# Two-layer recurrence on one core: the first three gates summed in two halves, the last two after the products

## The chip, the cores and the metric

One core of a Trainium2 chip runs the whole program; the other cores are idle. The metric is the device time of one execution in microseconds (us). The engines are TensorE (PE, with its weight loads shown as PEld), VectorE (DVE), ScalarE (ACT), GpSimd (POOL) and SyncE (SP).

## The reference, cut to what matters

A small network of several blocks is computed; the change touches only the fourth, a two-layer LSTM-like recurrence over 126 positions, batch 16, state 256.

```
def _run_layer(x_seq, Wx, Wh, b):
    gx = x_seq @ Wx + b                      # [128 or 256] -> 5 gates of 256
    def step(carry, gx_t):
        h, c, m = carry
        g = gx_t + h @ Wh
        i, f = sigmoid(g[:, 0:256]), sigmoid(g[:, 256:512])
        c_tilde = tanh(g[:, 512:768])
        o = sigmoid(g[:, 768:1024])
        m_new = tanh(g[:, 1024:1280])
        c_new = f * c + i * c_tilde
        h_new = o * tanh(c_new) + m_new
        return (h_new, c_new, m_new), h_new
h1 = _run_layer(x, Wx0, Wh0, b0)
h2 = _run_layer(h1, Wx1, Wh1, b1)            # then a dense layer on h2
```

The blocks before it (patch embedding, attention, a routed feed-forward net) and after it (a second routed net) are the same in both kernels.

## The kernel before

**Layout.** Features lie on the 128 partitions. The five gates of 256 make ten chunks of 128 features (`GCH = 10`); chunks 0 to 5 (`XCH = 6`) are the input, forget and candidate gates (called IFC), chunks 6 to 9 the output gate and the memory gate (OM). All numbers of a matmul are split into a high and a low fp16 part. A chunk of one step takes 32 columns of PSUM: 16 for the products with the high part and 16 for those with the low part, which VectorE adds. Two steps (`PAIR = 2`) share a pair of PSUM banks x and y: before the change x holds the six IFC chunks and y the four OM chunks. Layer 0 has four banks (named bank in the profile), layer 1 the other four (named quad), so each layer has two pairs that alternate.

**Order of the work.** Both layers run in one loop, layer 1 four steps behind layer 0 (`BEHIND = 4`). `wave` unrolls the first 8 and the last values of t and makes a hardware loop of 4 steps a turn for the 116 in between. In t = 4 to 125 both layers work; in each of these 122 steps the kernel goes through two mirrored halves, one in which layer 0's state is finished and its next matmuls start, and one for layer 1. This text calls each a half-step.

**TensorE** (`both` in `rec_pe`, order by hand): `own(0)`: wait for the high part of the state (`high0`), 12 matmuls with the low weights on IFC (L1475), wait for the whole state (`state0`), 12 with the high weights (L1468), signal `pre_x0`; then 8 and 8 for OM, signal `pre_y0`. Then fillers that don't depend on this step: on even t the bias of the next pair (2 matmuls, L1494) and 12 matmuls of `chunks`; on odd t 8 of `chunks` and 10 of `from_first`, the input product of layer 1. Then the same for layer 1, `own(1)`, followed by 2 and 12 (even t) or 18 (odd t) fillers of `from_first`. So a half-step holds 40 matmuls of its own and 14 or 18 fillers.

**VectorE** (`both` in `rec_dve`): for layer l, with l' the other layer, in this order: `sum_part` x of layer l (L1644, 192 values read, 96 written per partition), then for l' `new_state` (L1672, output gate times tanh of the cell), `store_state` (L1683 the high part, L1685 the whole in f32), `store_low` (L1690, the low part, which completes the state), then for l again `sum_part` y (L1644, 128 read, 64 written), `products` (L1652), `new_cell` (L1658). Eight instructions in a half-step. Each has a wait of its own in front.

**ScalarE** (`both` in `rec_act`): `gates_x` (L1582, tanh of IFC, waits for sum x), `gate_out` (L1587, sigmoid of the output gate, waits for sum y), `cell_of` (L1595, tanh of the new cell, waits for the cell), `memory` (L1590). The order in the queue is not altered by the change: the output gate already stands ahead of the cell.

**GpSimd** copies layer 1's state to a history (L1417) and splits the next two inputs (L1402, L1405), for which it waits on `pre_y0` of an earlier step.

Of the kernel before, what the change touches and what calls it, by code (L numbers as in the profile page):

```python
# [30 lines left out]
SEQ = PATCHES + WORDS  # L31
# [26 lines left out]
XCH = 3 * KH  # L58
XW = XCH * BATCH
# [35 lines left out]
def build(nc, taps_in, patches_in, txt_in, cols_in, const_in, dense_in, qkvw_in, outw_in, heads_in, w0_in,  # L95
# [6 lines left out]
    with ExitStack() as ctx:  # L102
# [1351 lines left out]
        def rec_pe(pe):  # L1454
# [3 lines left out]
            def chunk_at(l, q, m, first, steps):  # L1458

                x, y = pair_banks(l, q)  # L1460
                to, at = (x, m * 64) if m < XCH else (y, (m - XCH) * 64)
# [22 lines left out]

            IFC, OM, TOP = range(XCH), range(XCH, GCH), range(1)

# [4 lines left out]
            def start_bias(l, q):  # L1491
                x, y = pair_banks(l, q)
                for to, lo, n in ((x, 0, XCH), (y, XCH, GCH - XCH)):
# [4 lines left out]
            def own(l, n, u, states):  # L1498
# [6 lines left out]
                for k in range(KH):  # L1505
                    mm = high_weights(l, q, w + k, states[k], odd, IFC)
                mm.then_inc(sg(f"pre_x{l}"), 1)
# [5 lines left out]


            def connect(n, k):

                j, part = FC_PARTS[n]
                if k == 0:
                    pe.wait_ge(sg("fcw_in"), 16)
                    pe.wait_ge(sg("hist"), (j * BLK + part.stop + BATCH - 1) // BATCH)  # L1520
                    pe.wait_ge(sg("sum_x0"), SEQ - 2 if j < 2 else SEQ)
# [9 lines left out]
            chunks(0, 0, WX0, xcur_parts[:, 0], IFC).then_inc(sg("pre_x0"), 1)  # L1531
# [4 lines left out]
            def both(t, u):  # L1536
                q, odd = u // PAIR, u % PAIR
                if here(t, 1, SEQ - 1):
                    before = (u - 1) % 4
                    own(0, t, u, [hpair0[:, before // PAIR, k, before % PAIR:before % PAIR + 1] for k in range(KH)])  # L1540
# [6 lines left out]
                if odd and here(t, PAIR, SEQ + 1):  # L1547
                    from_first(q, 0, OM)
                    from_first(q, 1, TOP)
                if here(t, BEHIND + 1, SEQ + BEHIND - 1):  # L1550
                    own(1, t - BEHIND, u, [hpair1[:, 1 - odd, k:k + 1] for k in range(KH)])
                if here(t, PAIR, SEQ + 1):
# [10 lines left out]
                    else:  # L1563
                        for which, name in ((IFC[1:], "pre_x1"), (OM, "pre_y1")):
                            mm = from_first(q, 1, which)
                            if isinstance(t, int) and t == PAIR + 1:
                                mm.then_inc(sg(name), 1)
                for j, k in FC_AFTER.get(t, ()) if isinstance(t, int) else ():
# [8 lines left out]
        def rec_act(act):  # L1577
            act.activation(warm[:, :], warm[:, :], ACT.Sigmoid)

            def gates_x(l, n):  # L1580
                act.wait_ge(sg(f"sum_x{l}"), n)
# [38 lines left out]
        def rec_dve(dve):  # L1620
# [18 lines left out]
            def sum_part(l, n, u, name):  # L1639

                x, y = pair_banks(l, u // PAIR)
                src, first, count = (x, 0, XCH) if name == "x" else (y, XCH, GCH - XCH)
                dve.wait_ge(sg(f"pre_{name}{l}"), n)
# [3 lines left out]
                                  ).then_inc(sg(f"sum_{name}{l}"), 1)  # L1647
# [45 lines left out]
            def both(t, u):  # L1693
# [5 lines left out]
                if first_layer:  # L1699
                    sum_part(0, n0, u, "x")  # L1700
# [4 lines left out]
                if first_layer:  # L1705
                    sum_part(0, n0, u, "y")
# [4 lines left out]
                if first_layer:  # L1711
                    products(0, n0)
# [473 lines left out]
```

## Time and profile before

| | |
|---|---|
| median of 3 runs | 999.2 us (995.4 to 1002.92) |
| profiled execution, its own time | 1000.61 us |
| its span, first to last instruction | 998.8 us |
| busy over the span | PE 849.3 (85%), PEld 681.8 (68%), DVE 762.0 (76%), ACT 506.2 (51%), POOL 367.3 (37%) |
| the stage of the change, both layers at work | from about 492.8 to 892.6 us |

The rows further down come from this one profiled execution. In a timeline row stand start, duration, engine, line, operation, tiles written and read, partitions times elements, how many instructions were merged, and in brackets idle time of the engine before it with what ended it. A duration runs from an instruction's start to its result; two instructions on VectorE or ScalarE that don't wait for each other overlap, so what an engine is really taken up by is the distance from one start to the next.

### The profile page before, as it was taken

The page shows a single profiled execution, that of the slowest core. Times are in us where ns is not written, and L with a number is a line of the kernel's source. Part 1 is how long each engine was busy: PE and PEld are TensorE (multiplying, and loading weights), DVE is VectorE, ACT ScalarE, POOL GpSimd, SP SyncE. Part 2 cuts the span into 40 slices and gives each one's busy share as a digit, 9 for nine tenths or more (in the row PEclk, how much of TensorE's full clock was granted, in tenths as well). Part 3 has the DMA queues.
Part 4 walks back from the last instruction along what each step waited for, and adds up shares of the span by engine and source line. Part 5 has one row for each costly group of instructions (what it writes and reads, how often), then busy time and mean ns, then how long its engine had stood idle before and what let it go on. Part 6 is the DMA issues. An engine that isn't in the chain of part 4 may idle for free.

```text
span 998.8 us, 44167 instructions
## 1 busy us (share of the span) xinstructions
PE 849.3 (85%) x17239; PEld 681.8 (68%) x17239; DVE 762.0 (76%) x2780; ACT 506.2 (51%) x1605; POOL 367.3 (37%) x565
## 2 busy tenths in 40 slices
PE   4577777735999999995899999999999999998595
PEld 2246554513666666662699999999999999985263
DVE  4447897598877777677789999999999999987144
ACT  0435776701765555653455555555555555556083
POOL 0305664656677777760011111111111111100644
PEclk8767997755999999995899999999999999999697
DMA  7710002420122222225200000000000000002133
GB/s 235 293 37 1 1 1 76 152 68 25 37 76 79 79 78 78 77 47 171 93 4 0 0 0 0 0 0 0 0 0 0 0 0 0 0 3 65 42 100 113
DMA packets 30137, 50.64 MB, mean 51 GB/s; under 512 B 7969, under 2 KB 19161, under 8 KB 30074
## 3 DMA queue, kind: packets, MB, share of 16 engines
q1 hardware_dynamic: 23578, 36.95, 11.7%
q0 software_dynamic: 6496, 12.84, 4.8%
q8 instruction: 40, 0.66, 0.3%
q14 instruction: 23, 0.19, 0.1%
HBM read 38.40 MB, written 11.38 MB: 50 GB/s over the span
## 4 chain that ended last, share of the span: by engine, by line
DVE 29%; PE 6%; issue 6%; ACT 5%; POOL 4%; DMA 1%; DVEq 1%; SPq 0%; POOLq 0%
DVE post L1644 7%; ACT post L1595 5%; DVE post L1672 5%; DVE post L1683 4%; DVE post L1658 4%; DVE post L1652 3%; DVE post L1685 3%; POOL y_scratch L1783 2%; POOL x_scratch L1777 1%; DVE post L1690 1%; PE quad L1468 1%; PE quad L1475 1%; PE bank L1475 1%; PE bank L1468 1%; PE bank L1523 1%
## 5 line engine op out<-in xcount | busy, mean ns | idle before, releaser
L1475 PE MATMUL quad<-post,area 128*128 128x16 f16 (+1 forms) x3760 | 174.2, 172 | 6.8 <-DVE post L1683 6.8
L1468 PE MATMUL quad<-post,area 128*128 128x32 f16 (+1 forms) x3760 | 175.8, 182 | 0.1
L1417 POOL COPY post<-post 128x32 f32 (+1 forms) x126 | 29.8, 237 | 336.2 <-DVE post L1690 336.2
L1475 PEld LDWEIGHTS quad<-post,area 128*128 128x128 f16 x3760 | 136.5, 96 | 16.1 <-DVE post L1683 12.5
L1475 PE MATMUL bank<-post,area 128*128 128x16 f16 (+1 forms) x3130 | 135.5, 171 | 3.8 <-DVE post L1683 2.1
L1468 PE MATMUL bank<-post,area 128*128 128x32 f16 (+1 forms) x3130 | 138.2, 180 | 0.1
L1468 PEld LDWEIGHTS quad<-post,area 128*128 128x128 f16 x3760 | 133.9, 96 | 0.2 <-issue 0.2
L1587 ACT ACTIVATE post<-post 128x32 f32<-128x32 f32 x252 | 57.8, 229 | 147.6 <-DVE post L1644 147.2
L1475 PEld LDWEIGHTS bank<-post,area 128*128 128x128 f16 x3130 | 106.5, 96 | 10.3 <-DVE post L1683 2.8
L1468 PEld LDWEIGHTS bank<-post,area 128*128 128x128 f16 x3130 | 106.1, 96 | 0.8 <-issue 0.3
L892 POOL DMA_INDIRECT y_scratch<-area x78 | 81.3, 1042 | 31.4 <-issue 18.0
L887 POOL DMA_INDIRECT area<-x_scratch,area x78 | 78.7, 1010 | 28.1 <-issue 21.0
L1644 DVE TENSOR_REDUCE post<-bank 128x96 f32<-128x192 f32 x252 | 80.6, 320 | 10.4 <-PE bank L1468 10.1
L1076 ACT ACTIVATE area<-quad 128x512 f16<-128x512 f32 x78 | 46.6, 598 | 76.4 <-PE quad L971 76.3
L1582 ACT ACTIVATE post<-post 128x96 f32<-128x96 f32 x252 | 71.3, 283 | 26.3 <-DVE post L1644 23.8
L1644 DVE TENSOR_REDUCE post<-quad 128x96 f32<-128x192 f32 x252 | 80.6, 320 | 2.4 <-PE quad L1468 1.8
L1273 DVE TENSOR_TENSOR area<-quad,area 128x512 f16<-128x512 f32 x78 | 53.6, 688 | 29.0 <-ACT area L1076 28.7
L1595 ACT ACTIVATE post<-post 128x32 f32<-128x32 f32 x252 | 57.8, 229 | 33.5 <-DVE post L1658 2.2
L1289 DVE SCALAR_TENSOR_TENSOR area<-bank,area 128x512 f32<-128x512 f32 x78 | 53.7, 688 | 27.0 <-ACT area L1087 14.9
L961 PE MATMUL bank<-w0s,area 128*128 x156 | 60.4, 387 | 0.2
L962 PE MATMUL bank<-w0s,area 128*128 x156 | 60.1, 386 | 0.0
L963 PE MATMUL bank<-w0s,area 128*128 x156 | 60.1, 386 | 0.0
(337 smaller groups left out, 1938.6 us busy)
## 6 DMA issues: line engine op xcount, KB each, us to landing
w0s<-in_w SPq DMA_DIRECT2D x12, 768.0 KB
area<-in_rec SPq DMA_DIRECT2D x7, 640.0 KB
post<-y_scratch SPq DMA_DIRECT2D x8, 504.0 KB
area<-in_w SPq DMA_DIRECT2D x4, 768.0 KB
area<-in_f SPq DMA_DIRECT2D x2, 1024.0 KB, 7.6
area<-in_patches SPq DMA_DIRECT2D x1, 1488.4 KB
x_scratch<-post SPq DMA_DIRECT2D x1, 1472.0 KB, 7.2
area<-in_taps SPq DMA_DIRECT2D x1, 1350.0 KB
```

Of the source, the lines that this page charges most:

```text
L887: pool.indirect_dma_start(xg[:, i % XG, :], None, x_dram, bass.IndirectOffsetOnAxis(src_row[:, i:i + 1].bitcast(mybir.dt.uint32), 0)).then ...
L892: pool.indirect_dma_start(y_dram, bass.IndirectOffsetOnAxis(dst_row[:, i:i + 1].bitcast(mybir.dt.uint32), 0), y_sb[:, i % YR, :], None).th ...
L961: pe.matmul(out, xh, wh, start=True, stop=False, skip_group_check=True)
L962: pe.matmul(out, xl, wh, start=False, stop=False, skip_group_check=True)
L963: pe.matmul(out, xh, wl, start=False, stop=True, skip_group_check=True).then_inc(sg(name), 1)
L1289: dve.scalar_tensor_tensor(out=hid[:, i % 2, :], in0=up_bank(i), scalar=HID_SCALE / (H_SCALE * W_SCALE), in1=silu[:, i % 2, :], op0=ALU.mu ...
L1468: mm = pe.matmul(chunk_at(l, q, m, first, operand.shape[1]), rec_w[:, w, 0, m * P:(m + 1) * P], operand, start=False, stop=False, skip_gro ...
L1475: mm = pe.matmul(chunk_at(l, q, m, first, operand.shape[1])[:, :, 0, :], rec_w[:, w, 1, m * P:(m + 1) * P], operand[:, :, 0, :], start=Fal ...
L1582: act.activation(gates[:, l, 0:3 * SW], pre[:, l, 0:3 * SW], ACT.Tanh, scale=UNSCALE).then_inc(sg(f"gates{l}"), 1)
L1587: act.activation(gates[:, l, OUT:OUT + SW], pre[:, l, 3 * SW:4 * SW], ACT.Sigmoid, scale=UNSCALE)
L1595: act.activation(tanh_c[:, l], gates[:, l, CELL:CELL + SW], ACT.Tanh, scale=0.5).then_inc(sg(f"tanh_c{l}"), 1)
L1644: dve.tensor_reduce(pre[:, l, first * BATCH:(first + count) * BATCH].rearrange("p (m b) -> p m b", b=BATCH), src[:, 0:count * 64].rearrang ...
```

## The change

The two PSUM banks of a pair are filled differently: x now holds only chunks 0 to 2 (`BCH = 3`), y holds chunks 3 to 5 and, behind them, 6 to 9.

- TensorE: in `own`, the 12 high-weight matmuls on IFC are done in two parts, first the six of chunks 3 to 5 (`SOONER`), then the six of chunks 0 to 2 (`LATER`), each with a signal on `pre_x`. The 16 OM matmuls move to `own_rest`, behind the fillers, and `own_rest` first waits until VectorE has summed the first half ("a") of this step, because OM writes the bank that this sum reads. In `from_first` the order of the chunks is changed to match. Matmuls and their sizes are the same in number; only the bias's two are 96 and 224 columns in place of 192 and 128 (x and y hold 3 and 7 chunks).
- VectorE: `sum_part` x becomes two sums, "a" (chunks 3 to 5, bank y) and "x" (chunks 0 to 2, bank x), each 96 read and 48 written. The order after `store_low` is products, sum y, new cell in place of sum y, products, new cell. Nine instructions in a half-step in place of eight.
- ScalarE: only the value that `gates_x` waits for doubles.

```diff
+BCH = XCH // 2
@@ chunk_at
-                to, at = (x, m * 64) if m < XCH else (y, (m - XCH) * 64)
+                to, at = (x, m * 64) if m < BCH else (y, (m - BCH) * 64)
@@ rec_pe
+            LATER, SOONER = range(BCH), range(BCH, XCH)
@@ start_bias
-                for to, lo, n in ((x, 0, XCH), (y, XCH, GCH - XCH)):
+                for to, lo, n in ((x, 0, BCH), (y, BCH, GCH - BCH)):
@@ own
                 pe.wait_ge(sg(f"state{l}"), n)
-                for k in range(KH):
-                    mm = high_weights(l, q, w + k, states[k], odd, IFC)
-                mm.then_inc(sg(f"pre_x{l}"), 1)
+                for part in (SOONER, LATER):
+                    for k in range(KH):
+                        mm = high_weights(l, q, w + k, states[k], odd, part)
+                    mm.then_inc(sg(f"pre_x{l}"), 1)
+
+            def own_rest(l, n, u, states):
+
+                q, odd, w = u // PAIR, u % PAIR, (WH0, WH1)[l]
+                pe.wait_ge(sg(f"sum_x{l}"), n * 2 + 1)
                 for k in range(KH):
                     low_weights(l, q, w + k, states[k], odd, OM)
                 for k in range(KH):
                     mm = high_weights(l, q, w + k, states[k], odd, OM)
                 mm.then_inc(sg(f"pre_y{l}"), 1)
@@ connect
-                    pe.wait_ge(sg("sum_x0"), SEQ - 2 if j < 2 else SEQ)
+                    pe.wait_ge(sg("sum_x0"), 2 * (SEQ - 2 if j < 2 else SEQ))
@@ both (TensorE)
                 if odd and here(t, PAIR, SEQ + 1):
                     from_first(q, 0, OM)
                     from_first(q, 1, TOP)
+                if here(t, 1, SEQ - 1):
+                    own_rest(0, t, u, states0)
                 if here(t, BEHIND + 1, SEQ + BEHIND - 1):
-                    own(1, t - BEHIND, u, [hpair1[:, 1 - odd, k:k + 1] for k in range(KH)])
+                    own(1, t - BEHIND, u, states1)
...
-                        for which, name in ((IFC[1:], "pre_x1"), (OM, "pre_y1")):
+                        for which, name in ((OM, "pre_y1"), (SOONER, "pre_x1"), (LATER[1:], "pre_x1")):
                             mm = from_first(q, 1, which)
                             if isinstance(t, int) and t == PAIR + 1:
                                 mm.then_inc(sg(name), 1)
+                if here(t, BEHIND + 1, SEQ + BEHIND - 1):
+                    own_rest(1, t - BEHIND, u, states1)
@@ gates_x (ScalarE)
-                act.wait_ge(sg(f"sum_x{l}"), n)
+                act.wait_ge(sg(f"sum_x{l}"), n * 2)
@@ sum_part (VectorE)
-                src, first, count = (x, 0, XCH) if name == "x" else (y, XCH, GCH - XCH)
-                dve.wait_ge(sg(f"pre_{name}{l}"), n)
+                src, first, count = {"x": (x, 0, BCH), "a": (y, BCH, XCH - BCH), "y": (y[:, (XCH - BCH) * 64:], XCH, GCH - XCH)}[name]
+                if name == "y":
+                    dve.wait_ge(sg(f"pre_y{l}"), n)
+                else:
+                    dve.wait_ge(sg(f"pre_x{l}"), n * 2 - 1 if name == "a" else n * 2)
@@ both (VectorE)
                 if first_layer:
+                    sum_part(0, n0, u, "a")
                     sum_part(0, n0, u, "x")
...
                 if first_layer:
-                    sum_part(0, n0, u, "y")
+                    products(0, n0)
...
                 if first_layer:
-                    products(0, n0)
+                    sum_part(0, n0, u, "y")
                     new_cell(0, n0)
                 if second_layer:
+                    sum_part(1, n1, u, "a")
                     sum_part(1, n1, u, "x")
...
                 if second_layer:
-                    sum_part(1, n1, u, "y")
+                    products(1, n1)
...
                 if second_layer:
-                    products(1, n1)
+                    sum_part(1, n1, u, "y")
                     new_cell(1, n1)
```

## Rows read from the trace of the kernel before

**Rows 1.** Page, busy time of each engine; and the lines of the chain that ended last

```profile
PE 849.3 (85%) x17239; PEld 681.8 (68%) x17239; DVE 762.0 (76%) x2780; ACT 506.2 (51%) x1605; POOL 367.3 (37%) x565
...
DVE post L1644 7%; ACT post L1595 5%; DVE post L1672 5%; DVE post L1683 4%; DVE post L1658 4%; DVE post L1652 3%; DVE post L1685 3%; POOL y_scratch L1783 2%; POOL x_scratch L1777 1%; DVE post L1690 1%; PE quad L1468 1%; PE quad L1475 1%; PE bank L1475 1%; PE bank L1468 1%; PE bank L1523 1%
```

**Rows 2.** Windows, the two-layer stage: stretch, length, busy (instructions), PEclk, DMA share, GB/s

```profile
492.80:892.60 399.80, 392.63 (x13562) 379.83 (x13562) 364.92 (x1946) 209.26 (x973) 55.19 (x240) 1.00 0.00 0
```

**Rows 3.** Waits, 500 to 880 us: who waited for whom, us in total, times, longest

```profile
ACT post L1587 <- DVE post L1644: 139.8, 231, 0.7
...
DVE post L1644 <- PE bank L1468: 9.0, 30, 0.4
```

**Rows 4.** Timeline of VectorE, one half-step (layer 1's state, then layer 0's)

```profile
665.42 0.19 DVE L1683 SCALAR_TENSOR_TENSOR post<-post 128x32 f16<-128x32 f32 x1
665.53 0.18 DVE L1685 SCALAR_TENSOR_TENSOR post<-post 128x32 f32<-128x32 f32 x1
665.75 0.19 DVE L1690 TENSOR_TENSOR post<-post 128x32 f16<-128x32 f32 x1
665.86 0.28 DVE L1644 TENSOR_REDUCE post<-quad 128x64 f32<-128x128 f32 x1
666.06 0.21 DVE L1652 SCALAR_TENSOR_TENSOR post<-post 128x64 f32<-128x64 f32 x1
666.31 0.19 DVE L1658 SCALAR_TENSOR_TENSOR post<-post 128x32 f32<-128x32 f32 x1
666.50 0.36 DVE L1644 TENSOR_REDUCE post<-bank 128x96 f32<-128x192 f32 x1
666.79 0.19 DVE L1672 SCALAR_TENSOR_TENSOR post<-post 128x32 f32<-128x32 f32 x1
667.02 0.19 DVE L1683 SCALAR_TENSOR_TENSOR post<-post 128x32 f16<-128x32 f32 x1
```

**Rows 5.** Timeline of ScalarE, the same half-step

```profile
666.17 0.23 ACT L1587 ACTIVATE post<-post 128x32 f32<-128x32 f32 x1 [0.59 <-DVE post L1644]
666.53 0.23 ACT L1595 ACTIVATE post<-post 128x32 f32<-128x32 f32 x1
666.67 0.21 ACT L1590 ACTIVATE post<-post 128x32 f32<-128x32 f32 x1
666.89 0.28 ACT L1582 ACTIVATE post<-post 128x96 f32<-128x96 f32 x1
```

**Rows 6.** Timeline of the weight loads, the same half-step, 58 of them

```profile
665.66 0.36 PEld L1475 LDWEIGHTS bank<-post,area 128*128 128x128 f16 x12
665.99 0.37 PEld L1468 LDWEIGHTS bank<-post,area 128*128 128x128 f16 x12
666.29 0.27 PEld L1475 LDWEIGHTS bank<-post,area 128*128 128x128 f16 x8
...
666.69 0.17 PEld L1475 LDWEIGHTS bank<-post,area 128*128 128x128 f16 x4
...
667.14 0.10 PEld L1468 LDWEIGHTS quad<-post,area 128*128 128x128 f16 x1
667.26 0.36 PEld L1475 LDWEIGHTS quad<-post,area 128*128 128x128 f16 x12
```

**Rows 7.** Timeline of the matmuls, the twelve with high weights on IFC

```profile
666.00 0.47 PE L1468 MATMUL bank<-post,area 128*128 128x32 f16 x12
```

**Rows 8.** Timeline of VectorE where its loop turns

```profile
662.83 0.19 DVE L1658 SCALAR_TENSOR_TENSOR post<-post 128x32 f32<-128x32 f32 x1
663.33 0.36 DVE L1644 TENSOR_REDUCE post<-bank 128x96 f32<-128x192 f32 x1 [0.30 <-PE bank L1468]
663.60 0.18 DVE L1672 SCALAR_TENSOR_TENSOR post<-post 128x32 f32<-128x32 f32 x1
```

**Rows 9.** Groups by line and form, VectorE, 500 to 880 us: the two kinds of sum

```profile
L1644 DVE TENSOR_REDUCE post<-bank 128x96 f32<-128x192 f32 x115 | 41.1, 357 | 9.1 <-PE bank L1468 9.0
L1644 DVE TENSOR_REDUCE post<-quad 128x64 f32<-128x128 f32 x116 | 32.7, 282 | 0.0
```

**Rows 10.** Timeline of VectorE after the recurrence: two instructions that both read PSUM

```profile
927.83 1.28 DVE L1992 SCALAR_TENSOR_TENSOR post<-bank,post 126x512 f16<-126x512 f32 x2
```

**Rows 11.** Timeline of VectorE in a step where layer 1 works alone

```profile
893.64 0.19 DVE L1683 SCALAR_TENSOR_TENSOR post<-post 128x32 f16<-128x32 f32 x1
...
894.72 0.69 DVE L1644 TENSOR_REDUCE post<-quad 128x96 f32<-128x192 f32 x2 [0.56 <-PE quad L1468]
895.42 0.23 DVE L1652 SCALAR_TENSOR_TENSOR post<-post 128x64 f32<-128x64 f32 x1
895.68 0.19 DVE L1658 SCALAR_TENSOR_TENSOR post<-post 128x32 f32<-128x32 f32 x1
```

More of the change, by code:

```diff
@@ L1530, in rec_pe @@
             pe.wait_ge(sg("xcur"), PAIR)
-            chunks(0, 0, WX0, xcur_parts[:, 0], IFC).then_inc(sg("pre_x0"), 1)
+            chunks(0, 0, WX0, xcur_parts[:, 0], SOONER).then_inc(sg("pre_x0"), 1)
+            chunks(0, 0, WX0, xcur_parts[:, 0], LATER).then_inc(sg("pre_x0"), 1)
+            pe.wait_ge(sg("sum_x0"), 1)
             chunks(0, 0, WX0, xcur_parts[:, 0], OM).then_inc(sg("pre_y0"), 1)
@@ L1537, in both @@
                 q, odd = u // PAIR, u % PAIR
+                before = (u - 1) % 4
+                states0 = [hpair0[:, before // PAIR, k, before % PAIR:before % PAIR + 1] for k in range(KH)]
+                states1 = [hpair1[:, 1 - odd, k:k + 1] for k in range(KH)]
                 if here(t, 1, SEQ - 1):
-                    before = (u - 1) % 4
-                    own(0, t, u, [hpair0[:, before // PAIR, k, before % PAIR:before % PAIR + 1] for k in range(KH)])
+                    own(0, t, u, states0)
                 if here(t, 0, SEQ - 3):
@@ L1646, in sum_part @@
                                       "p (m s g b) -> p s m b g", m=count, s=PAIR, g=2)[:, u % PAIR], AX, ALU.add
-                                  ).then_inc(sg(f"sum_{name}{l}"), 1)
+                                  ).then_inc(sg(f"sum_y{l}" if name == "y" else f"sum_x{l}"), 1)
             def products(l, n):
@@ L1718, in both @@
                     store_state(0, n0, u)
+                if first_layer:
                     store_low(0, n0, u)
                 if second_layer:
-                    sum_part(1, n1, u, "y")
+                    products(1, n1)
                 if isinstance(t, int) and t < NBLK:
```

## The prediction

> **What bounds the kernel now.** I read the page first. No engine is busy for the whole span, and the chain that ended last names VectorE's recurrence lines before all others, with ScalarE's L1595 among them [rows 1]. Then the windows: the stage with both layers at work lasts 399.8 us and VectorE starts 1946 instructions in it, which at eight a half-step is 243; by the code it is 122 steps of two, 244 [rows 2]. One half-step so takes 1.64 us. In this stage the matmuls look 98% busy, but that is a reading of overlapping matmuls, so it settles nothing: the timelines do.
>
> The timeline of VectorE shows what a half-step is made of. I write all times from H, the start of the high part (L1683), and take distances from start to start [rows 4]: high to whole state 0.11, to low part 0.22, to sum y 0.11, to products 0.20, to cell 0.25, to new state (L1672) 0.48 to 0.49, to the next high 0.22 to 0.23. The sum is 1.60 (665.42 to 667.02). What counts is why each distance has its length. 0.11 and 0.20 are VectorE's own pace for instructions that don't wait for each other; they fit elements read / 0.96 per ns plus 0.07 to 0.08 (32: 0.11; 128: 0.20; 192: 0.27 to 0.28 from the sum x to L1672 [rows 4, 8]). 0.22 and 0.25 are a full duration plus about 0.04: the next instruction needs this one's result. The 0.48 from cell to new state is ScalarE: the cell is done at +0.19, L1595 starts at +0.22, takes 0.23, and L1672 starts 0.03 to 0.04 later [rows 4, 5]. VectorE fills this gap with the sum x of the other layer.
>
> TensorE is close behind. The high part is done at H+0.19, the low-weight matmuls start at H+0.24; the state is done at H+0.52, the high-weight ones start at H+0.57 and end at 666.47 = H+1.05 [rows 6, 7]; sum x starts at H+1.08. Its 58 weight loads of the half-step go at 25 to 27 ns each: 12 in 0.33 (with a few hundredths of waiting for the state), 12 in 0.30, 16 in 0.40, 18 fillers in 0.48 to 0.50 (666.69 to 667.17, and the next load could start by 667.19). That is 1.52, and the next start is 1.60 after the first [rows 6]. So TensorE has 0.08 to spare, and in half-steps with 14 fillers rather more. It is granted 1.00, its 2.4 GHz level, throughout [rows 2]; nothing here alters that.
>
> Once a turn of the loop VectorE loses about 0.3: cell to sum x takes 0.50, and cell to new state 0.77 [rows 8]; 30 such waits make 9.0 us [rows 3]. 244 x 1.60 + 28 x 0.28 = 398, which is the stage. So the model of before closes.
>
> **The change, part by part, for one half-step.**
>
> *Order sum y, products, cell becomes products, sum y, cell.* Before: 0.11 + 0.20 + 0.25 = 0.56 from low part to cell. After: low part to products 0.11, products (64 elements) to sum y 0.07 + 0.075 = 0.145, sum y to cell 0.20, in which the products' result (0.21 + 0.04 = 0.25) has come: 0.455. Saved 0.105. This takes a wait for its own result off VectorE. The products need ScalarE's `gates_x` earlier by 0.20; sum x ends at H+1.44, the gates run to about H+1.75, the products are wanted at H+1.60+0.44: cover of 0.29 [rows 4, 5].
>
> *The output gate against the cell on ScalarE.* The output gate starts 0.31 after the start of sum y [rows 4, 5]. Before, the cell's tanh came 0.36 later still. Now the cell starts 0.20 after sum y, so its tanh could start at 0.42, but the output gate has only just started at 0.31, and ScalarE's pace for two such is 0.14 (L1595 to L1590 [rows 5]): 0.45. Cost 0.03, cell to new state becomes 0.52. Bounds: 0 and, if a sigmoid and a tanh don't overlap at all, 0.31 + 0.23 - 0.42 = 0.12. I take 0.03, by the nearest rows.
>
> *One sum more.* 192 elements in one piece cost 0.27 to 0.28; two of 96 cost 2 x (0.10 + 0.07) = 0.34. They lie in the gap that ScalarE sets. With C for the cell's start: "a" at C+0.14, "x" at C+0.31, VectorE free at C+0.48; wanted at C+0.52. Cost nothing, with 0.04 of cover; without it, all of the 0.06 to 0.07. That two sums from PSUM overlap like others is not seen before, the nearest is a pair of L1992, 512 read each, 1.28 for both at 0.67 each: 0.61 apart, 0.53 + 0.08 [rows 10]. Upper bound: no overlap, "a" takes its whole duration, 0.282 less 32 x 1.17 ns = 0.245 by [rows 9], then VectorE is free at C+0.55 and 0.03 is lost.
>
> The Trainium skill speaks against this part: VectorE: DVE Perf Modes (section on the TRN2 errata) gives an instruction that reads PSUM 120 cycles beside its elements, and its rules for kernel authors say to minimize the count of operations. By that figure, taken as an estimate, two sums would hold VectorE for 0.45, and the new state would start at C+0.56 to 0.59; the half-step 1.565 to 1.595 and the time 992 to 999. The rows above, at 0.07 to 0.08 beside the elements, don't agree with it as a pace.
>
> *TensorE, first half sooner.* "a" needs only six of the high-weight matmuls: H+0.57 + 0.125 + 0.19 = H+0.89, so it may start at H+0.92; VectorE wants it at C+0.11 with C = H+0.79, that is H+0.90. "x" may start at H+1.08 and is wanted at H+1.09. Both fit.
>
> *TensorE, the new wait.* Behind `own`'s 24 matmuls (to H+0.87) now come the fillers (to H+1.36), then `own_rest`. It waits for "a", done at H+0.92 + 0.25, seen 0.05 later: H+1.22. The fillers cover it by 0.14. Queued behind it are 16 matmuls (to H+1.76), and behind these the next `own`, which the next half-step wants at H+1.77. Cost nothing, but cover of 0.01 to 0.04 only. Bound: a second start from a wait costs 0.05 like the others, then TensorE's loop is 1.57.
>
> *Sum y* of this layer needs `own_rest`: last matmul H+1.76 + 0.19, wanted at H+1.53 + 0.585 = H+2.11. Cover 0.15. GpSimd's wait on `pre_y0` is for a step further back, and its input is used by fillers that run 0.40 earlier; no DMA is moved.
>
> *Where the loop turns*, the 0.3 before the first sum stays; "a" comes late, `own_rest(0)` with it, but VectorE is later still. Nothing. In steps with one layer alone (four at each end) the cell starts at H+2.04 [rows 11]; by the same distances after the change it is H+2.04 to 2.08. Nothing.
>
> **The sum.** 0.22 + 0.11 + 0.22 + 0.11 + 0.145 + 0.20 + 0.52 = 1.525, against 1.60. TensorE's loop, 1.52, just lets it. 0.075 x 244 = 18.3 us. From the profiled execution's own 1000.6 that is 982.3; this one lay 1.4 above the median of 999.2. I predict 982.
>
> **Rivals.**
>
> *More (975).* ScalarE's order costs nothing: 0.105 x 244 = 25.6 off. For it, the output gate is off the path of before by a third of a microsecond; against it, the queue is in order. 8%.
>
> *Less, by the sums (about 990).* Two PSUM sums in a row don't overlap: 0.245 + 0.17 from C+0.14 puts the new state at C+0.55, 0.045 x 244 = 11 us are left. For it: no such pair stands in the recurrence before; against it, the pair that overlaps [rows 10]. 10%. The rule of the skill quoted above would make this rival true, and larger.
>
> *Less, by TensorE (about 993).* Its loop is 1.57, the new wait costing 0.05: 0.03 x 244 = 7 us are left. For it: two engines would sit within 0.01 of each other, and neither can smooth the other's hiccups. 14%.
>
> *No change (999).* Two such losses, or a sigmoid before a tanh that doesn't overlap (1.62 in place of 1.525). 10%.
>
> *Slower (from 1009).* TensorE becomes the bound. Its order now has three waits a half-step in place of two, each of which empties what it had lined up. Where the waits of before ended, it lost 0.05. If `own_rest` resumed 0.125 or more late in every half-step, its loop would be over 1.645 and the kernel 0.045 x 244 = 11 us slower; it decides from 0.08, where 1.60 is reached. For it: 1.52 of 1.60 is used already. Against it: fillers of 0.48 lie between the last matmul that "a" needs and the wait. 9%.
>
> **How the numbers follow.** My forecast (977 to 987) has 49%. Faster by over 1% (about what a measurement here can tell from no change), below 989.2, takes it, "more", and some 6 of the 24 of the two "less": 0.63. Within 1%: their rest, no change: 0.28. Slower 0.09. The range reaches from "more" to no change, 975 to 999; the forecast's own is 977 to 987.
>
> **What would show it.** In the profile after, half-steps of 1.52 to 1.53 from L1683 to L1683; products to sum y 0.145; cell to new state 0.52 with the cell's tanh 0.14 behind the output gate; two sums 0.17 apart; no idle time of weight loads ahead of `own_rest`. Wrong: sums 0.25 apart; weight loads of 58 in over 1.55 with VectorE idle ahead of "a"; idle TensorE that ends on the sum.

## The result and the profile after

| | before | after |
|---|---|---|
| median | 998.0 us (4 runs) | 976.2 us (4 runs, 974.8 to 978.0) |
| ratio | 1 | 0.9763, 95% interval 0.9731 to 0.9794 |
| profiled execution's own time | 1000.6 us | 974.8 us |
| its span | 998.8 us | 973.0 us |
| from the high part of layer 0's fourth state to the last of the two-layer stage | 402.4 us | 378.0 us |
| the same, median distance of neighbouring high parts | 1.60 us | 1.50 us (mostly 1.49 and 1.50) |

The change is faster by 2.4% (2.2% by the quotient of the two medians). The forecast was 982, 18.3 us off the profiled execution of before. The direction was right, but the gain was larger: 24.4 us in the stage of the change. What was measured, 974.8 in the profiled execution and 976.2 in the median, lies just below the forecast's own range of 977 to 987. The rest of this text is on why.

The windows of the stage (length, busy of PE, PEld, DVE, ACT, POOL with instructions, granted clock) against [rows 2]:

```profile
491.20:866.60 375.40, 373.27 (x13577) 369.22 (x13578) 348.18 (x2188) 182.62 (x973) 53.44 (x240) 0.99 0.00 0
```

399.8 us became 375.4, 24.4 less, with 2188 instructions on VectorE, nine for each of 243 half-steps. The span fell by 25.8. Of the other 1.4, 2.3 us came ahead of the recurrence (its first high part stands at 479.79 in place of 482.04), where nothing was changed and where the other runs of this text on chips as fast there lie between 478.3 and 482.9, and 1.2 went the other way in the steps with one layer alone. So the change itself is worth about 23 us.

The timeline of VectorE after, one half-step, to be read against [rows 4]:

```profile
644.00 0.19 DVE L1701 SCALAR_TENSOR_TENSOR post<-post 128x32 f16<-128x32 f32 x1
644.11 0.18 DVE L1703 SCALAR_TENSOR_TENSOR post<-post 128x32 f32<-128x32 f32 x1
644.32 0.19 DVE L1708 TENSOR_TENSOR post<-post 128x32 f16<-128x32 f32 x1
644.43 0.22 DVE L1670 SCALAR_TENSOR_TENSOR post<-post 128x64 f32<-128x64 f32 x1
644.57 0.28 DVE L1662 TENSOR_REDUCE post<-bank 128x64 f32<-128x128 f32 x1
644.77 0.18 DVE L1676 SCALAR_TENSOR_TENSOR post<-post 128x32 f32<-128x32 f32 x1
644.92 0.42 DVE L1662 TENSOR_REDUCE post<-quad 128x48 f32<-128x96 f32 x2
645.26 0.19 DVE L1690 SCALAR_TENSOR_TENSOR post<-post 128x32 f32<-128x32 f32 x1
645.49 0.19 DVE L1701 SCALAR_TENSOR_TENSOR post<-post 128x32 f16<-128x32 f32 x1
```

From the high part H: state instructions as before, products at H+0.43, sum y at +0.57, cell at +0.77, the first half sum at +0.92, both halves together 0.42 from start to result, the new state at +1.26, the next high part at +1.49. The two sums overlap: 0.42 less one's 0.25 puts them 0.17 apart.

ScalarE in the same half-step, against [rows 5]: output gate, tanh of the cell, memory, gates.

```profile
644.88 0.23 ACT L1602 ACTIVATE post<-post 128x32 f32<-128x32 f32 x1 [0.72 <-DVE post L1662]
645.02 0.21 ACT L1610 ACTIVATE post<-post 128x32 f32<-128x32 f32 x1
645.14 0.21 ACT L1605 ACTIVATE post<-post 128x32 f32<-128x32 f32 x1
645.38 0.28 ACT L1597 ACTIVATE post<-post 128x96 f32<-128x96 f32 x1
```

TensorE's weight loads, against [rows 6]: twelve low, twelve high, fillers, the sixteen of `own_rest`, the next twelve.

```profile
644.25 0.37 PEld L1476 LDWEIGHTS quad<-post,area 128*128 128x128 f16 x12
644.57 0.36 PEld L1469 LDWEIGHTS quad<-post,area 128*128 128x128 f16 x12
644.86 0.17 PEld L1476 LDWEIGHTS quad<-post,area 128*128 128x128 f16 x4
...
645.35 0.28 PEld L1476 LDWEIGHTS quad<-post,area 128*128 128x128 f16 x8
645.55 0.27 PEld L1469 LDWEIGHTS quad<-post,area 128*128 128x128 f16 x8
645.75 0.37 PEld L1476 LDWEIGHTS bank<-post,area 128*128 128x128 f16 x12
```

There is no gap ahead of `own_rest` (645.35): the fillers cover its wait. TensorE goes round in 1.50, without rest: 0.32 + 0.29 + 0.49 + 0.40. Accordingly the page's chain that ended last now follows TensorE nearly all the way:

```profile
PE 41%; DVE 4%; POOL 3%; DMA 2%; issue 2%; ACT 1%; ACTq 0%; SPq 0%; POOLq 0%; DVEq 0%
PE quad L1469 11%; PE quad L1476 9%; PE bank L1469 9%; PE bank L1476 8%; POOL x_scratch L1798 2%; POOL y_scratch L1804 1%; DMA post<-y_scratch 1%; PE bank L1496 1%; PE quad L1496 1%; DVE post L1662 1%; DVE post L1318 0%; ACT area L1983 0%; PE bank L1530 0%; PE quad L1019 0%; DVE post L1926 0%
```

This reads as if TensorE's amount of work were now the bound. The experiments show that it isn't alone: two other chains lie within 0.02 of it.

### The profile page after: what moved, and what is told of

Same layout as the page of the kernel before. It is cut to its first block, busy times and chain, and to the rows that moved or that the text cites. A ratio compares the mean times of both kernels' runs of the same rounds, so it can differ in the third digit from the quotient of the medians.

```text
span 973.0 us, 44506 instructions
## 1 busy us (share of the span) xinstructions
PE 828.1 (85%) x17239; PEld 669.5 (69%) x17239; DVE 743.7 (76%) x3032; ACT 478.0 (49%) x1605; POOL 364.0 (37%) x565
## 4 chain that ended last, share of the span: by engine, by line
PE 41%; DVE 4%; POOL 3%; DMA 2%; issue 2%; ACT 1%; ACTq 0%; SPq 0%; POOLq 0%; DVEq 0%
PE quad L1469 11%; PE quad L1476 9%; PE bank L1469 9%; PE bank L1476 8%; POOL x_scratch L1798 2%; POOL y_scratch L1804 1%; DMA post<-y_scratch 1%; PE bank L1496 1%; PE quad L1496 1%; DVE post L1662 1%; DVE post L1318 0%; ACT area L1983 0%; PE bank L1530 0%; PE quad L1019 0%; DVE post L1926 0%
## 5 line engine op out<-in xcount | busy, mean ns | idle before, releaser
L1469 PE MATMUL quad<-post,area 128*128 128x32 f16 (+1 forms) x3760 | 176.1, 182 | 0.0
L1476 PEld LDWEIGHTS quad<-post,area 128*128 128x128 f16 x3760 | 144.7, 96 | 5.7 <-DVE post L1701 3.4
L1602 ACT ACTIVATE post<-post 128x32 f32<-128x32 f32 x252 | 57.8, 229 | 182.3 <-DVE post L1662 182.3
L1418 POOL COPY post<-post 128x32 f32 (+1 forms) x126 | 27.1, 215 | 312.5 <-DVE post L1708 312.5
L1469 PE MATMUL bank<-post,area 128*128 128x32 f16 (+1 forms) x3130 | 138.4, 181 | 0.7 <-issue 0.7
L1469 PEld LDWEIGHTS quad<-post,area 128*128 128x128 f16 x3760 | 137.6, 96 | 0.0
L1476 PEld LDWEIGHTS bank<-post,area 128*128 128x128 f16 x3130 | 110.3, 96 | 9.0 <-DVE post L1701 3.2
L1469 PEld LDWEIGHTS bank<-post,area 128*128 128x128 f16 x3130 | 106.9, 96 | 0.9 <-issue 0.9
L1662 DVE TENSOR_REDUCE post<-bank 128x48 f32<-128x96 f32 x378 | 89.0, 263 | 10.6 <-PE bank L1469 10.1
L1662 DVE TENSOR_REDUCE post<-quad 128x48 f32<-128x96 f32 x378 | 88.9, 263 | 1.5 <-PE quad L1469 1.0
L1670 DVE SCALAR_TENSOR_TENSOR post<-post 128x64 f32<-128x64 f32 x252 | 55.0, 218 | 3.1 <-ACT post L1597 3.1
```

The lines of the kernel that those rows point to most:

```text
L1469: mm = pe.matmul(chunk_at(l, q, m, first, operand.shape[1]), rec_w[:, w, 0, m * P:(m + 1) * P], operand, start=False, stop=False, skip_gro ...
L1476: mm = pe.matmul(chunk_at(l, q, m, first, operand.shape[1])[:, :, 0, :], rec_w[:, w, 1, m * P:(m + 1) * P], operand[:, :, 0, :], start=Fal ...
L1602: act.activation(gates[:, l, OUT:OUT + SW], pre[:, l, 3 * SW:4 * SW], ACT.Sigmoid, scale=UNSCALE)
L1662: dve.tensor_reduce(pre[:, l, first * BATCH:(first + count) * BATCH].rearrange("p (m b) -> p m b", b=BATCH), src[:, 0:count * 64].rearrang ...
L1670: dve.scalar_tensor_tensor(out=prod[:, l], in0=gates[:, l, 0:2 * SW], scalar=1.0, in1=gates[:, l, CAND:CAND + 2 * SW], op0=ALU.add, op1=AL ...
```

## The experiments

Each kernel was run beside the kernel before on the same chip, and ratios are to that. The first four were on a chip where the work ahead of the recurrence takes some 40 us longer in every kernel and the work behind it 7 to 10 (the kernel before: 1051 us), so whole times of different groups must not be compared; the half-steps may. The edits are shortened: they stand for both layers, and `...` marks lines left out. "Stage" is the distance in the table above: before 402.4, after 378.0.

### The order alone

The kernel before, with VectorE's order changed; sum x stays whole.

```diff
-    sum_part(l, n, u, "y")
-    products(l, n)
+    products(l, n)
+    sum_part(l, n, u, "y")
     new_cell(l, n)
```

> The kernel before with one part of the change alone: products, sum y, new cell in this order; sum x stays one piece, TensorE as before. Theory: the cell comes 0.11 us earlier after the high part H (H+0.78 in place of H+0.89), but sum x can't start before TensorE's twelve high-weight matmuls are done, H+1.08, and takes 0.28; the new state then starts at H+1.36, the half-step is 1.58 in place of 1.60: 0.02 x 244 = 5 us off, about 993. Rival: the order alone carries the gain: 0.10 x 244 = 25 us off, about 973.

Ratio 0.9903 (0.9862 to 0.9943); median half-step 1.57, stage 391.3: 11 us less. Twice the 5 that were expected, under half of the rival's 25. 0.03 in each half-step make 7 of the 11; most of the rest fell where the loop turns, whose half-step went from 1.93 to 1.73, which the expectation had left out. The timeline of VectorE (with one row of TensorE) shows the reason given:

```profile
641.24 0.19 DVE L1683 SCALAR_TENSOR_TENSOR post<-post 128x32 f16<-128x32 f32 x1
...
641.81 0.47 PE L1468 MATMUL bank<-post,area 128*128 128x32 f16 x12
...
642.01 0.18 DVE L1658 SCALAR_TENSOR_TENSOR post<-post 128x32 f32<-128x32 f32 x1
...
642.32 0.36 DVE L1644 TENSOR_REDUCE post<-bank 128x96 f32<-128x192 f32 x1
...
642.59 0.18 DVE L1672 SCALAR_TENSOR_TENSOR post<-post 128x32 f32<-128x32 f32 x1
...
642.81 0.19 DVE L1683 SCALAR_TENSOR_TENSOR post<-post 128x32 f16<-128x32 f32 x1
```

The cell is at H+0.77, yet sum x starts only at H+1.08, when TensorE's twelve matmuls end (642.28), and the new state follows 0.27 later. ScalarE's tanh has long been done. The chain through TensorE has taken the place of ScalarE's.

### The split alone

The kernel after, with VectorE's order put back to sum y, products, cell.

```diff
-    products(l, n)
-    sum_part(l, n, u, "y")
+    sum_part(l, n, u, "y")
+    products(l, n)
     new_cell(l, n)
```

> The kernel after with the old order on VectorE (sum y, products, new cell); the two half sums, the banks and TensorE's order stay. Theory: the cell is back at H+0.89, cell to new state is 0.49 as ScalarE sets it, the half-step 1.60: about 998, no gain. Rival: the split carries the gain, since TensorE's signal comes sooner: under 985.

Ratio 1.0063 (1.0033 to 1.0093), median half-step 1.60, stage 407.2. No gain, as expected, and a small loss; it stands where the loop turns (2.01 in place of 1.93) and in the step in which layer 1 joins (4.27 in place of 2.76), of which more below. With the order alone at -11 us and the split alone at +5 in the stage, both together give -24: the split is worth 13 us, but only once the cell is earlier; the order is worth 29 once the sum is split. The ratios say the same: -1.0%, +0.6%, and -2.4% for both. Neither part can be priced by itself.

### `own_rest` ahead of the fillers

```diff
     own(0, t, u, states0)
+    own_rest(0, t, u, states0)
...  (the fillers)
-    own_rest(0, t, u, states0)
```

The same for layer 1.

> The kernel after with own_rest directly behind own, ahead of the fillers. Theory: TensorE then has nothing to do from H+0.87 until the first half sum is done and seen at H+1.22, 0.35 idle in each half-step; 16 loads to H+1.62, 18 fillers to H+2.11, half-step about 1.86 in place of 1.495: 0.36 x 244 = 89 us more than after, about 1065. Rival: the wait is short anyway and the place doesn't matter: within 10 us of 976.

Ratio 1.0501 (1.040 to 1.060, from two runs); half-step 1.85, stage 454.0, 76 us more than after. Expected 1.86 and 89. The expectation took the 1.86 against 1.495, a half-step of after without turns; here a turn costs almost nothing more (1.86 to 1.89), so the means are 1.86 against 1.55. Weight loads in one half-step:

```profile
701.64 0.37 PEld L1469 LDWEIGHTS bank<-post,area 128*128 128x128 f16 x12
702.31 0.27 PEld L1476 LDWEIGHTS bank<-post,area 128*128 128x128 f16 x8 [0.30 <-DVE post L1660]
```

The new wait is real, and the fillers are what hides it: the 16 loads start 0.67 behind the start of the twelve, where without a wait it is 0.30 (665.99 to 666.29 in [rows 6]).

### The output gate behind the cell

```diff
     gates_x(l, n)
-    gate_out(l, n)
     cell_of(l, n)
+    gate_out(l, n)
     memory(l, n)
```

The signal that `new_state` waits for moves with it, from the tanh to the output gate.

> The kernel after with ScalarE's output gate behind the tanh of the cell (the signal for new_state moves to the output gate). Theory: the tanh starts at cell+0.22, the output gate 0.14 later and takes 0.21, the new state starts 0.03 behind it at cell+0.60 in place of +0.49: 0.11 x 244 = 27 us more, about 1003. Rival: VectorE's sums or TensorE alone set the half-step and ScalarE's order costs nothing: 976.

Ratio 1.0002 (0.9964 to 1.0040) to the kernel before, where the kernel after has 0.9763: 2.4% of 1000, 24 us, against 27 expected. Half-step 1.60, stage 400.0. The tanh starts at 702.25, the output gate at 702.39 for 0.21, the new state at 702.63: cell+0.59. With ScalarE's order as it is, the gate ahead of the cell, this is 0.49. So ScalarE's path has next to no room: 0.10 more on it is 0.10 more in the half-step.

### Less work for TensorE, less for VectorE, both

Left out in the first: the low-weight matmuls of `own_rest`, eight in a half-step. In the second: sum y reads only the products with the high part of the state. The third has both.

```diff
 # own_rest
-    for k in range(KH):
-        low_weights(l, q, w + k, states[k], odd, OM)
 # sum_part
+    values = ...    (what the sum read before)
+    if name == "y":
+        values = values[:, :, :, 0:1]
```

> The kernel after; left out: the 8 low-weight matmuls of own_rest in each half-step (the low parts of the output and memory gates' recurrent weights are not applied). TensorE has 0.20 us less in each half-step of 1.49 to 1.51. Theory A (several chains tie at 1.49 to 1.50: TensorE's own work; ScalarE's path from sum y to new state; the chain from the state through TensorE's twelve matmuls and the two sums): no gain, within 4 us of after. Theory B (TensorE's amount of work alone binds, as the chain that ended last would have it): 10 us or more off.

> The kernel after; left out: sum y reads 64 values in place of 128 (the products with the state's low part are not added for the output and memory gates). Sum y takes 0.067 us less on the path through cell and tanh. Theory A: TensorE's work, at 1.48 to 1.51, holds the half-step: 0 to 5 us off. Rival C (VectorE and ScalarE alone bind): 0.067 x 244 = 16 us off.

> The kernel after with both omissions: no low-weight matmuls in own_rest, sum y reads 64 values. Theory A: now the third chain holds: high part H, state done H+0.52, matmuls H+0.57 to H+1.04, second half sum H+1.08, new state 0.17 later at H+1.25, high 0.22 later: 1.475 in place of 1.495, 5 us off. Rival (only two chains were tied): 0.06 x 244 = 15 us off.

| | ratio to before | median half-step | stage |
|---|---|---|---|
| after | 0.9763 (0.9731 to 0.9794) | 1.50 | 378.0 |
| less TensorE | 0.9696 (0.9664 to 0.9727) | 1.50 | 375.7 |
| less VectorE | 0.9734 (0.9710 to 0.9757) | 1.49 | 375.3 |
| both | 0.9668 (0.9648 to 0.9687) | 1.48 | 372.8 |

0.20 us less work for TensorE in each half-step brings 2.3 us in the stage, not 49. So its work alone is not the bound, whatever the chain of the page says: in the run with less of it, TensorE now waits for the high part (L1699 here) where in after it went on without a gap.

```profile
641.32 0.37 PEld L1476 LDWEIGHTS quad<-post,area 128*128 128x128 f16 x12 [0.22 <-DVE post L1699]
```

The ratio of this run lies 0.67% below that of after, which is more than the stage accounts for. About half of it is the kernel before that ran beside it, 1001.7 in place of 998.0; the medians themselves, 973.3 and 976.2, differ by 2.8 us, near the stage's 2.3. So the stage is what I go by. "Both" falls out as theory A said, by the size of the stage: 5.2 us, about the sum of the two alone. That ScalarE's path was relieved shows too: its tanh ends 0.10 before the new state starts, in place of 0.03 (medians over the half-steps of 500 to 850 us).

### Three omissions, of which the third was the wrong one

As "both", and three of the six high-weight matmuls of chunks 0 to 2 are left out, by which the second half sum could start sooner.

```diff
-    for k in range(KH):
+    for k in range(KH if part is SOONER else 1):
         mm = high_weights(l, q, w + k, states[k], odd, part)
```

> The kernel after with three omissions: no low-weight matmuls in own_rest, sum y reads 64 values, and three of the six high-weight matmuls of chunks 0 to 2 left out of own (half of the state is not applied there), so that the second half sum may start 0.075 us sooner. Theory A (three chains tied, each omission alone worth at most 5 us): half-step 1.42 to 1.43, 0.065 to 0.075 x 244 = 16 to 18 us off, more than the omissions alone together. Theory B or C (one chain alone): the same as that chain's omission alone.

Ratio 0.9648 (0.9609 to 0.9687), half-step 1.48, stage 372.8: the third omission brought nothing, and theory A as I had put it was wrong. The timeline says what I had overlooked:

```profile
641.43 0.19 DVE L1701 SCALAR_TENSOR_TENSOR post<-post 128x32 f16<-128x32 f32 x1
...
642.00 0.39 PE L1469 MATMUL bank<-post,area 128*128 128x32 f16 x9
...
642.13 0.18 DVE L1676 SCALAR_TENSOR_TENSOR post<-post 128x32 f32<-128x32 f32 x1
...
642.36 0.42 DVE L1663 TENSOR_REDUCE post<-bank 128x48 f32<-128x96 f32 x2
642.39 0.21 ACT L1608 ACTIVATE post<-post 128x32 f32<-128x32 f32 x1
...
642.70 0.18 DVE L1690 SCALAR_TENSOR_TENSOR post<-post 128x32 f32<-128x32 f32 x1
```

The cell is at H+0.70 now and ScalarE's tanh is done at H+1.17 (642.60), but the first half sum still starts at H+0.93: six matmuls from H+0.57 take until H+0.89. From there 0.17 + 0.17 lead to the new state at H+1.27. It is the first half, not the second, on which this chain hangs.

### The right three matmuls, alone and with the rest

The same omission in chunks 3 to 5 in place of 0 to 2.

```diff
-    for k in range(KH):
+    for k in range(1 if part is SOONER else KH):
         mm = high_weights(l, q, w + k, states[k], odd, part)
```

> The kernel after; left out: three of the six high-weight matmuls of chunks 3 to 5 in own (half of the state is not applied there), so the first half sum may start 0.075 us sooner. New theory E, from the rows of the two runs with omissions: the half-step is the chain high part, state done (H+0.52), six matmuls, first half sum at H+0.93, second 0.17 later, new state 0.17 later, high part 0.22 later: 1.49; ScalarE's path comes within 0.01 of it. Then this alone gives little, because ScalarE's path (new state at H+1.26) takes over: half-step 1.48 to 1.49, 0 to 3 us less than after (ratio to before 0.973 to 0.977). Rival: ScalarE's path has room and the chain alone binds: 0.06 x 244 = 15 us less than after (0.962).

> The kernel after with three omissions: the same three high-weight matmuls of chunks 3 to 5, no low-weight matmuls in own_rest, sum y reads 64 values. Theory E: all that ties is relieved; new state at H+1.20 to 1.21, half-step 1.42 to 1.44: 0.055 to 0.07 x 244 = 13 to 17 us less than after (ratio to before 0.959 to 0.963), and clearly more than with chunks 0 to 2 in place of 3 to 5 (0.9648, half-step 1.48). Rival: another chain, not yet seen, holds 1.48: the same 0.965.

Alone: ratio 0.9752 (0.9716 to 0.9789), half-step 1.50, stage 377.6: nothing, since ScalarE's path takes over: the first half sum starts at H+0.87 in place of 0.93, but the new state still waits until 0.03 after the end of the tanh (medians as above). With the two other omissions: ratio 0.9629 (0.9592 to 0.9666), half-step 1.44, stage 363.9, 14.1 us less than after and 8.9 less than with the wrong three. In this kernel:

```profile
700.50 0.19 DVE L1701 SCALAR_TENSOR_TENSOR post<-post 128x32 f16<-128x32 f32 x1
...
701.20 0.23 DVE L1676 SCALAR_TENSOR_TENSOR post<-post 128x32 f32<-128x32 f32 x1
...
701.36 0.42 DVE L1663 TENSOR_REDUCE post<-quad 128x48 f32<-128x96 f32 x2
...
701.73 0.19 DVE L1690 SCALAR_TENSOR_TENSOR post<-post 128x32 f32<-128x32 f32 x1
```

The first half sum is at H+0.86, as reckoned. This half-step is one of 1.46; most are 1.43. The chains are shown to be level by the sum: 0.4 us for the one, 5.2 for the other two, 14.1 for the three. How far this needs TensorE's omission is not shown: no run relieves ScalarE's path and the chain of the sums together while `own_rest` keeps all its matmuls. That TensorE's work is the third level chain rests on its rows, which have no idle time in after.

### Longer turns of the loop

The kernel after, complete. First all engines with 8 and with 16 steps in a turn, to save turns at about 0.28 us each.

```diff
-    with eng.Fori(2, SEQ // 4) as i:
-        for u in range(4):
-            both(i * 4 + u, u)
+    with eng.Fori(1, SEQ // 8) as i:
+        for u in range(8):
+            both(i * 8 + u, u % 4)
...
```

> The kernel after, complete, with 8 steps in a turn of the hardware loop in place of 4 on each engine; t = 120 to 123 move to the unrolled end. Each turn costs about 0.28 us; 13 turns remain in place of 28 or so, 14 or 15 fewer: 4 us less than after (ratio to before 0.972). Rival: the loss belongs to fetching instructions, and a body twice as long gives it back or more (0.976 or above).

> The kernel after, complete, with 16 steps in a turn and the first 16 and the last 19 steps unrolled; 5 turns back remain in place of 28: 6 us less than after (ratio to before 0.970). Rival: as for 8 steps, longer straight code costs in fetching what the turns cost: 0.976 or above.

Ratios 1.0104 (1.0074 to 1.0133) and 1.0251 (1.0204 to 1.0298): slower than the kernel before, and by 34 and 49 us against after. The rival was right, by far more than it said. The half-step's median is 1.50 in both; the loss stands in single stops. Weight loads in the run with 8, 500 to 860 us (who waited for whom, us in total, times, longest):

```profile
PEld bank L1476 <- issue: 27.1, 12, 4.4
PEld quad L1476 <- issue: 2.9, 8, 0.6
PEld bank L1469 <- issue: 2.6, 5, 0.5
PEld quad L1469 <- issue: 1.8, 5, 0.5
```

"issue" means that TensorE waited for nothing the profile shows. With 4 steps a turn these rows add up to 0.9 us; with 8 they are 34.4, which is the whole loss in the stage (412.2 against 378.0). With 8 steps the body holds 896 matmuls, each with a weight load. The DMA queues point to the cause, for they list the transfers of instructions by themselves. From 530 to 860 us, inside the loop, the kernel after has none; the run with 8 steps has 55 on one queue.

```profile
DMA packets 0, 0.00 MB, mean 0 GB/s; under 512 B 0, under 2 KB 0, under 8 KB 0
```

```profile
q8 instruction: 55, 0.90, 1.2%
```

So the longer body is brought in anew in every turn, about nine packets of 16 KB in each, and the short one is not. The long stop comes once a turn, and in the one shown here two of the packets start at 611.6 and 612.4, just as it begins:

```profile
615.96 0.40 PEld L1476 LDWEIGHTS bank<-post,area 128*128 128x128 f16 x12 [4.37 <-issue]
```

That a stop waits for just these packets no row names; that of the kernels here only those that fetch inside the loop stop so is shown.

Then VectorE and ScalarE with 8 or 16 steps a turn, TensorE and GpSimd left at 4.

```diff
+    turn = 4 if eng is nc.tensor else 8
...  (the unrolled steps ahead of the loop)
-    with eng.Fori(2, SEQ // 4) as i:
-        for u in range(4):
-            both(i * 4 + u, u)
+    with eng.Fori(max(1, 8 // turn), SEQ // turn) as i:
+        for u in range(turn):
+            both(i * turn + u, u % 4)
...  (the unrolled steps behind it)
```

> The kernel after, complete; VectorE and ScalarE loop over 8 steps a turn, TensorE and GpSimd over 4 as before. Theory F (the 0.3 us idle ahead of the first half sum is VectorE's own turn): half of the 28 turns go, 14 x 0.28 = 4 us less than after, about 0.4% (ratio to before 0.972); the idle time that ends on TensorE's L1469 falls from 8 to about 4 us in 500 to 860. Rival G (it is TensorE's turn): the same time as after, 0.976.

> The kernel after, complete; VectorE and ScalarE loop over 16 steps a turn and have the first 16 unrolled, TensorE and GpSimd loop over 4. Theory F: 22 turns fewer, 6 us less than after (ratio to before 0.970). Rival G: as after, 0.976. Rival H: VectorE too has to fetch the longer body and stops as TensorE did: above 0.98.

With 8: ratio 0.9729 (0.9707 to 0.9751), stage 374.3, 3.7 us less than after. VectorE's waits of 500 to 860 us, first after, then this kernel:

```profile
DVE post L1662 <- PE bank L1469: 8.0, 30, 0.4
```

```profile
DVE post L1663 <- PE bank L1470: 4.4, 16, 0.5
```

30 waits became 16, as theory F had it, while TensorE's turns stayed as they were: though the profile puts the waits down to TensorE's L1469, they come from VectorE's own turn. (ScalarE's loop was lengthened with VectorE's, but by the code the first half sum waits for no signal of ScalarE.) This version is the fastest complete one here; its gain over after is seen in the stage and the waits, while the intervals of the ratios overlap. With 16: 0.9955 (0.9933 to 0.9977), stage 393.7; now VectorE itself stops 5 times on "issue" in this stretch, 14.9 us in all and up to 3.0. That was rival H. Again instructions are transferred inside the loop (530 to 860 us), on another queue than TensorE's run used, where the run with 8 steps on VectorE has one packet:

```profile
q14 instruction: 30, 0.25, 0.2%
```

## Why the prediction was off

**Right: the direction, the place and most of the terms.** All of the gain sits in the 244 half-steps. Order of sum y, products, cell: low part to cell was to fall from 0.56 to 0.455, it fell to 0.45 (644.32 to 644.77). Products to sum y was taken as 0.145 and is 0.13 to 0.14. Two PSUM sums overlap and lie 0.17 apart, 0.10 for the elements and 0.07 beside them, as the pair of [rows 10] had it; the fixed part that the Trainium skill gives for an instruction reading PSUM (VectorE: DVE Perf Modes, section on the TRN2 errata) is not the pace of two in a row here. The fillers cover the new wait, by the order given for it, and the run with `own_rest` moved ahead shows what it costs without them (1.85, expected 1.86). The rivals "less", "no change" and "slower" did not happen.

**The step that failed: "the output gate against the cell on ScalarE", 0.03. It measured nothing.** The tanh did start 0.14 behind the output gate, 0.25 after the cell in place of 0.22, as written. But I let it then take the 0.23 of [rows 5], where it starts on an idle ScalarE. Started 0.14 behind another it takes 0.21, like L1590 in that same group, which I had in front of me. Cell to new state is 0.49 to 0.50, not 0.52. The running distances bring 1.49 to 1.50 where I had 1.525: 0.10 x 244 = 24.4 us, and the stage is shorter by 24.4. That the two agree to the digit is chance: two half-steps of each turn fell by more (1.93 to 1.76 where the loop turns, and 1.63 to 1.50), and the step in which layer 1 joins grew by 1.27.

**TensorE's loop was 0.02 too long in the same sum.** I had it at 1.52 and wrote that it "just lets" the 1.525. Its parts measured 0.32 + 0.29 + 0.49 + 0.40 = 1.50, and over the half-steps without a turn it keeps up with 1.50 on average. Had 1.52 been right, the half-step could not have gone below it, and the time not below 981. Nor is there "rather more" to spare in half-steps with 14 fillers: they take 0.46 (641.87 to 642.33) where 18 take 0.49.

So my rival "more" gave the right time, 975, with the right statement, that this order costs nothing, though what it costs by starting late it gets back by being shorter. That it came out is partly luck: I had priced it without TensorE's loop, which by my own 1.52 forbade it. Had the order really cost nothing to the start, nothing more would have come of it, since two other chains stand at the same place.

**What I had not seen: the chain through TensorE and both sums.** I checked "a" and "x" each against the time at which VectorE wants them, and found them to fit, but I did not add up the chain: state done H+0.52, matmuls from H+0.57, six of them done H+0.89, first sum H+0.92, second +0.17, new state +0.17, high part +0.23: 1.49. In the kernel before the same chain, with twelve matmuls and one sum, is 1.08 + 0.27 + 0.22 = 1.57, only 0.03 under ScalarE's 1.60; the order alone ran into it at 1.57. That is why the change needs both parts: the order shortens the chain through cell and tanh, the split the one through TensorE, and each alone meets the other. After it, TensorE's work (1.48 to 1.50), ScalarE's path (1.49 to 1.50) and this chain (1.49) are level. For the last two the omissions show it: 0.4 and 5.2 us alone, 14.1 together; for TensorE's work its rows do. The 0.01 to 0.04 of cover that I had counted were used up by the shorter half-step, and this cost nothing, because none of the three then had to wait for another.

**Where the loop turns**: VectorE's waits are 30 of 8.0 us in all where they were 30 of 9.0, so nearly what was forecast; in the distance of high parts a turn costs 0.26 over the other half-steps where it was 0.33. That it is VectorE's own turn was shown only afterwards.

**The step in which layer 1 joins** took 4.03 in place of 2.76, which the prediction had not looked at. `own_rest` stands behind the fillers, and here the fillers wait for GpSimd, which splits the next input only after VectorE has made it; sum y waits for `own_rest`:

```profile
491.57 0.34 PE L1476 MATMUL bank<-post,area 128*128 128x32 f16 x6 [0.63 <-POOL post L1406]
...
492.70 0.29 DVE L1662 TENSOR_REDUCE post<-bank 128x64 f32<-128x128 f32 x1 [1.09 <-PE bank L1469]
```

The fillers hide the new wait only as long as they can run themselves.

**Steps with one layer alone** took 1.2 us more over the seven of them, 0.17 each, not 0 to 0.04. In the one shown the products (869.32) wait for the gates, sum y waits for `own_rest`, and the cell follows, where before sum y had been done in the meantime.

```profile
868.55 0.42 DVE L1662 TENSOR_REDUCE post<-quad 128x48 f32<-128x96 f32 x2 [0.41 <-PE quad L1469]
...
869.17 0.35 PE L1469 MATMUL quad<-post,area 128*128 128x32 f16 x8
...
869.32 0.23 DVE L1670 SCALAR_TENSOR_TENSOR post<-post 128x64 f32<-128x64 f32 x1 [0.35 <-ACT post L1597]
869.56 0.29 DVE L1662 TENSOR_REDUCE post<-quad 128x64 f32<-128x128 f32 x1
869.77 0.18 DVE L1676 SCALAR_TENSOR_TENSOR post<-post 128x32 f32<-128x32 f32 x1
```

The cell is at H+2.15 (H = 867.62), not at H+2.04 to 2.08: the second half sum ends at H+1.35, the gates run to H+1.66, and the products start at H+1.70, where before they started at H+1.78; 0.08 earlier, and 0.24 + 0.21 behind them in place of 0.26. I had set down 0.145 + 0.20 for these two, the pace in the full stage. But `own_rest` stands behind 14 fillers here too: its last matmul ends at 869.52, and sum y starts 0.04 later.

**What stays open**: whether the other two chains alone, relieved together, would bring the 14 us with TensorE's work left whole; and what decides at which length of the body instructions are fetched anew in every turn, between 4 and 8 steps on TensorE and between 8 and 16 on VectorE.

## What to carry to other kernels

In a software pipeline of two interleaved recurrences, write down every chain that leads from one state to the next, the one through each engine, and compare their sums; a change to one chain gains only down to the next, and two changes that are worth little alone can be worth much together. A new wait is free as long as other work fills the time up to it: put the dependent matmuls behind the independent ones, not ahead; and look for the steps in which the independent ones have to wait themselves. Read the duration of an instruction from a row in which it follows its neighbour as closely as it will after the change. Check each rival against every bound that the forecast itself names.

## What the runs showed of the hardware that was not expected

- An activation of 32 elements takes 0.23 us when ScalarE was idle before and 0.21 when it starts 0.12 to 0.14 behind another; the same is seen for a tanh behind a sigmoid. In the run with the right three omissions 45 tanhs start 0.15 behind the gate, and these take 0.23.
- With 896 matmuls in the body of the hardware loop in place of 448, TensorE stops once a turn for up to 4.4 us (with shorter stops of the same row 27.1 us in 12 times over 360 us), and instructions are transferred in every turn (55 packets from 530 to 860 us in place of none). VectorE with 16 steps in its turn stops for up to 3.0 us (30 packets), with 8 it doesn't.
- A turn of VectorE's loop costs 0.26 to 0.3 us here (16 waits in place of 30, 3.7 us less in the stage), though the profile names TensorE as the releaser.
